# Loading the first head's operands inside the projection stage, and spreading L2 norms in fp32

## The chip, the cores and the metric

The kernel runs on one core of one Trainium2 chip. The metric is the time of one execution in microseconds of device time. Engines are named as in the profile: PE (TensorE matmuls), PEld (its weight loads), DVE (VectorE), ACT (ScalarE), POOL (GpSimd), SP (SyncE, which here issues every DMA). A DMA's time "to landing" runs from its issue to its completion.

## What is computed

Two layers run one after the other on an activation `x` of shape (2, 2048, 256) in float32. Each layer is `x = x + attention(layernorm(x)) * silu(ffn(layernorm(x)))`. There are 16 heads of width 16.

```python
# layer 0, attention: distance weights, values gated
q2, k2 = sum(Q*Q), sum(K*K)                       # per token and head
dist = sqrt(max(q2 + k2.T - 2 Q K.T, 0))
W = (1e-4 + dist) ** -2
W = W / (1e-4 + sum(W))
out = X + (G * (W V)) W_out + b_out
# layer 1, attention: cosine weights
Q, K = Q / max(norm(Q), 1e-6), K / max(norm(K), 1e-6)   # per token and head
c = clip(Q K.T, -0.999, 0.999)
W = max(1 - arccos(c) / pi, 1e-6) ** 16
W = W / (sum(W) + 1e-6)
out = (W V) Wo + bo
```

The feed-forward of each layer multiplies by ternary weights (relu squared and a low-rank term in layer 0, relu and biases in layer 1).

## The kernel before

The program is a sequence of phases, and each is one block of five engine programs with semaphores between them: `constants_phase`, then for each layer `weights_phase`, `norm_phase`, `projection_phase`, an attention phase (`distance_phase` for layer 0, `cosine_phase` for layer 1) and `output_phase`. A phase ends when all five engine programs have ended; then a short block clears its semaphores (L139 and before), and only then does the next phase begin. SP's program in a phase is one ordered list of DMA issues and waits. So a DMA that a phase needs at its start can't be issued before the phase before it has wholly ended.

**Projection.** `projection_phase` goes over the 4096 tokens in 8 blocks of 512 (`TB`), the first four of which are the first batch entry. In a block PE computes the transposed Q and K features in four tiles `ft` of 128 features (L602, two fp32 128x512 matmuls each, into the first half of `psS`), the values (and in layer 0 the gates) of four token tiles (L583, into `psM`), and the sums of squares per head (`norms`, L575, into `psO`). ACT copies each tile to `proj` (L638 or L641) and squares it (L643). DVE cuts each fp32 tile into three bf16 parts (`split_parts`, L485 to L488, two casts and two subtractions, each waiting for the one before); the parts go into one of two buffers `parts[ft % 2]`, and SP stores them to DRAM (`qk_parts`, L539). The split of a tile first waits until the store two tiles back has landed, since it overwrites that buffer. In layer 0 DVE also adds biases to values and gates (L700, L702) and splits the norms (stored at L549); after all of PE's projection work POOL sets rows 96 to 127 of all four stacks to one (L740, four memsets). SP's order in a block is: four stores of parts, the values' store (L542), in layer 0 the gates' (L545) and four stores of norm parts (L549).

In layer 1 ACT turns the sums of squares into inverse norms (L656), and they have to be spread from 8 rows per tile to 128 features. DVE clamps them (L716) and cuts them into three bf16 parts that lie in three groups of rows (L717 to L720, a chain of four); PE multiplies the parts by a bf16 selection matrix (`expand`, L592, a 32-row matmul), and DVE multiplies the projected tile by the result (L724) and splits it. In PE's order the expansion of tile `ft - 1` of block `i - 1` follows the projection of tile `ft` of block `i`, for `ft` of 1 and more, and the last follows the values.

**Attention.** For each of 32 pairs of head and batch entry (`n`), SP loads `q_stack[b]` and `k_stack[b]` (6 DMAs of 64 KB each from `qk_parts`, and in layer 0 one more for norm rows: 14 DMAs in layer 0, 12 in layer 1), then the values into `v_tile[b]`, then the feed-forward's input. PE computes scores from the stacks (L861, L1179), 16 key tiles for a pair; everything after runs on lanes of a ring. With two stacks of each kind, the loads of pair `n + 2` wait until pair `n` is done.

**Memory that is shared.** The projection's weights lie in the stacks' memory: `wqk` in `k_stack[0]`, `wvg` in `k_stack[1]`, the selection matrices `sels` in `q_stack[1]`, so no stack can be loaded while the projection runs. `woT`, needed in the output phase, lies in `q_stack[0]`.

Of the kernel before, what the change touches and what calls it, by code (L numbers as in the profile page):

```python
# [53 lines left out]
class Mem:  # L54

    def __init__(self, nc, ctx):
# [25 lines left out]
        self.woT = self.q_stack[0][:, :].bitcast(F32)[:, 0:KD * D].rearrange("p (k d) -> p k d", k=KD)  # L83
        self.wqk = self.k_stack[0][:, :].bitcast(F32).rearrange("p (k n) -> p k n", k=KD)
        self.wvg = self.k_stack[1][:, :].bitcast(F32)
        self.sels = self.q_stack[1][:, :].bitcast(F32)[:, 0:P + NCOL]
        self.later = self.q_stack[1][:, :].bitcast(F32)[:, P + NCOL:P + NCOL + 2]
        self.psS = [ctx.enter_context(nc.psum_tensor(f"psS{i}", [P, 1024], F32)) for i in range(2)]
# [106 lines left out]
def load_projection(sp, m, io, L, loaded):  # L195

    vg_w = 2 * D if L == 0 else D
    sp.dma_start(m.wqk, io[f"wqk{L}"].rearrange("(k p) n -> p k n", p=P)).then_inc(loaded, 16)
    sp.dma_start(m.wvg[:, 0:KD * vg_w].rearrange("p (k n) -> p k n", k=KD),
                 io[f"wvg{L}"].rearrange("(k p) n -> p k n", p=P)).then_inc(loaded, 16)  # L200
    sp.dma_start(m.sels[:, 0:NCOL], io["sel"]).then_inc(loaded, 16)
    sp.dma_start(m.sels[:, NCOL:NCOL + P], io["selT"]).then_inc(loaded, 16)
    if L == 1:
        sp.dma_start(m.later, io["later"]).then_inc(loaded, 16)
    return 64 + 16 * L

# [284 lines left out]
def projection_phase(nc, m, io, L):  # L491
# [12 lines left out]
    selT = m.sels[:, NCOL:NCOL + P]  # L504
    selT16 = m.work[:, 12032:12032 + P // 2].bitcast(BF16)
    r_parts = m.work[:, 11520:11776].bitcast(BF16)
    r_rest = m.area(10240, 512)
    r_high = m.work[:, 11776:12032].bitcast(BF16)
    projs = [m.area(at, NQK, 512) for at in (4096, 12288)]
# [6 lines left out]
    n_parts = m.work[:, 10752:11520].bitcast(BF16).rearrange("p (a t) -> p a t", a=3)  # L516
    r_norm = m.area(10752, 512)
    n_loads = 2
    with Phase(nc) as ctx:
# [5 lines left out]
        s_st = sems(nc, ctx, pre, "stored0", "stored1")  # L525
        s_xT, s_vst, s_ones = sems(nc, ctx, pre, "xT_stored", "values_stored", "stack_ones")
        block = ctx.block()

        @block.sync
        def _(sp):  # L530
# [29 lines left out]
        def _(pe):  # L560
            pe.sem_inc(s_nm, 1)
            if L == 1:
                pe.wait_ge(s_bias, 1)
            if L == 0:
# [22 lines left out]
            def expand(i, ft):  # L587
# [3 lines left out]
                rows = slice(ft * NCOL, (ft + 1) * NCOL)  # L591
                nc.tensor.matmul(m.psS[ft % 2][:, 512:1024], selT16[rows, :], r_parts[rows, :], start=True, stop=True)\  # L592
                    .then_inc(s_e, 1)

            for i in range(TB):
                if L == 1:
                    values(i, range(2))
                for ft in range(NQK):
# [5 lines left out]
                    if L == 0:  # L605
                        values(i, (ft,))
                    elif i > 0 and ft > 0:
                        expand(i - 1, ft - 1)
                if L == 1:
                    values(i, (2, 3))  # L610
                    if i > 0:
                        expand(i - 1, NQK - 1)
                norms(i)
# [50 lines left out]
        def _(dve):  # L664
# [7 lines left out]

            per_block = NQK * 3 + (3 if L == 0 else 4)
            chain_n = [0]
            if L == 1:
                nc.vector.tensor_copy(selT16, selT).then_inc(s_bias, 1)
            if L == 0:
# [5 lines left out]
            def dve_block(i, proj):  # L683
# [49 lines left out]
        if L == 0:  # L733
            @block.gpsimd
            def _(pool):
                pool.wait_ge(s_proj, NQK * TB)
                pool.wait_ge(s_vps, NQK * TB)
                pool.wait_ge(s_nm, TB + 1)
                for stack in m.q_stack + m.k_stack:
                    nc.gpsimd.memset(stack[ROWS:P, :], 1.0).then_inc(s_ones, 1)  # L740
                pool.wait_ge(s_ones, 2 * B)

def distance_phase(nc, m, io):
# [33 lines left out]
    with Phase(nc) as ctx:  # L778
# [12 lines left out]
        def _(sp):  # L791
# [9 lines left out]
            for n in range(TILES):  # L801
                h, b = n // B, n % B
                if n >= B:

                    sp.wait_ge(s_qk, 2 * KT * (n - 1))
                tok = slice(b * T, (b + 1) * T)
                for side, stack in ((0, m.q_stack[b]), (1, m.k_stack[b])):
                    for g, pr in enumerate(PRODUCTS):
                        at = h * DH + side * D
                        sp.dma_start(stack[g * DH:(g + 1) * DH, :], io["qk_parts"][pr[side], at:at + DH, tok])\  # L810
                            .then_inc(s_stk[b], 16)
                    at = ROWS + 3 * side
                    sp.dma_start(stack[at:at + 3, :], io["norm_parts"][:, h + HEADS * side, tok]).then_inc(s_stk[b], 16)
                if n >= B:

                    sp.wait_ge(s_pv, KT * (n - 1))
                sp.dma_start(m.v_tile[b][:, :, 0:DH], views["v_store"][:, b, :, h, :]).then_inc(s_vt[b], 16)
                if n > 0:
# [30 lines left out]
        def _(pe):  # L849
            def scores(g):  # L850
                n, kt = g // KT, g % KT
                b = n % B
                if kt == 0:
                    pe.wait_ge(s_stk[b], 16 * loads * (n // B + 1))
                for half in range(2):
# [10 lines left out]
            def weighted(g):  # L866
                n, kt = g // KT, g % KT
                b = n % B
                if kt == 0:
                    pe.wait_ge(s_vt[b], 16 * (n // B + 1))  # L870
                    if n >= B:
# [182 lines left out]
def cosine_phase(nc, m, io):  # L1054
# [45 lines left out]
    with Phase(nc) as ctx:  # L1100
# [12 lines left out]
        def _(sp):  # L1113
# [8 lines left out]
            for n in range(TILES):  # L1122
                h, b = n // B, n % B
                if n >= B:

                    sp.wait_ge(s_qk, 2 * KT * (n - 1))
                tok = slice(b * T, (b + 1) * T)
                for side, stack in ((0, m.q_stack[b]), (1, m.k_stack[b])):
                    for g, pr in enumerate(PRODUCTS):
                        at = h * DH + side * D  # L1130
                        sp.dma_start(stack[g * DH:(g + 1) * DH, :], io["qk_parts"][pr[side], at:at + DH, tok])\
                            .then_inc(s_stk[b], 16)
                if n >= B:

                    sp.wait_ge(s_pv, KT * (n - 1))
                sp.dma_start(m.v_tile[b][:, :, 0:DH], v_view[:, b, :, h, :]).then_inc(s_vt[b], 16)
                if n > 0:
# [30 lines left out]
        def _(pe):  # L1168
            def scores(g):
                h, b, kt = g // UNITS, g % UNITS // KT, g % KT  # L1170
                if kt == 0:
                    pe.wait_ge(s_stk[b], 16 * loads * (h + 1))
                for half in range(2):
# [10 lines left out]
            def weighted(g):  # L1184
                h, b, kt = g // UNITS, g % UNITS // KT, g % KT
                j, p = batch_of(g)
                if kt == 0:
                    pe.wait_ge(s_vt[b], 16 * (h + 1))
                    if h > 0:
# [353 lines left out]
def layout(inputs):  # L1543
# [8 lines left out]
    sel = np.zeros((P, NCOL), np.float32)  # L1552
    for part in range(3):
        sel[np.arange(P), part * FH + np.arange(P) // DH] = 1.0
    later = np.zeros((NQK, NCOL, 2), np.float32)
    later[:, FH:3 * FH, 0] = -1.0
    later[:, 2 * FH:3 * FH, 1] = -1.0
    arrays = {
# [10 lines left out]
        "ident": np.eye(P, dtype=np.float32), "sel": sel, "selT": np.tile(sel.T, (NQK, 1)),  # L1569
        "later": later.reshape(P, 2),  # L1570
    }
# [15 lines left out]
```

## Time and profile before

| | us |
|---|---|
| three runs | 6657.21, 6659.45, 6663.84 (median 6659.45) |
| the profiled execution | 6664.82 |
| its span in the profile | 6663.0 |
| busy in the span | ACT 6192.9 (93%), DVE 5861.2 (88%), POOL 4185.4 (63%), PE 3922.0 (59%) |
| projection, layer 0 / layer 1 | about 92 to 230 / 2261 to 2416 |
| distance / cosine phase begins | 231.6 / 2417.8 |

In a timeline each row has the start, the duration, the engine, the line and operation, what it writes and reads, how many were merged (`x4`), and in brackets how long the engine was idle before it and what ended that. SPq is SP issuing a DMA; its duration is the issue alone. A row that merges several goes from the first's start to the last's end, waits between them included. Matmul ends are modelled and can overlap the next start.

### The profile page before, as it was taken

The numbers are of one execution on the slowest core, as the hardware profiler recorded it, in microseconds if no ns is written. First come the engines' busy times: TensorE is split into PE (matmuls) and PEld (weight loads), VectorE is DVE, ScalarE is ACT, GpSimd is POOL, SyncE is SP. The second block draws the span as 40 slices with busy tenths as digits, with TensorE's granted clock in tenths as the row PEclk, the third lists the DMA queues.
The fourth block names the chain that finished last, engine by engine and source line by source line (L and its number), as shares of the span: only waits on it lengthen the run. The fifth ranks groups of instructions, "written<-read, shape, count | busy, mean of one in ns | idle before, by whom it ended". The sixth has DMA issues, their size and how long they took to land. (4 is left out here: it accounts for less than half of the span.)

```text
span 6663.0 us, 49227 instructions
## 1 busy us (share of the span) xinstructions
PE 3922.0 (59%) x17040; PEld 1374.0 (21%) x17040; DVE 5861.2 (88%) x5938; ACT 6192.9 (93%) x1955; POOL 4185.4 (63%) x1127
## 2 busy tenths in 40 slices
PE   6787778777777754544444454444445444454545
PEld 3222222222222420211111121111112111111213
DVE  7776767766777789999999999999999999999997
ACT  3699999999998449999999999999999999999996
POOL 0399999999996006565565656565565656556563
PEclk8888888888888865665556565655666565565657
DMA  3211111111112320000000000000000000000003
GB/s 138 85 27 27 20 27 25 27 27 23 24 27 60 138 76 6 15 8 9 8 15 9 8 16 8 9 8 15 9 8 16 8 9 8 15 9 8 15 6 104
DMA packets 448273, 183.51 MB, mean 28 GB/s; under 512 B 348102, under 2 KB 429913, under 8 KB 446762
## 3 DMA queue, kind: packets, MB, share of 16 engines
q1 hardware_dynamic: 448042, 180.50, 10.8%
q8 instruction: 136, 2.23, 0.1%
q14 instruction: 95, 0.78, 0.0%
HBM read 108.33 MB, written 72.09 MB: 27 GB/s over the span
## 5 line engine op out<-in xcount | busy, mean ns | idle before, releaser
L1387 POOL TENSOR_TENSOR work<-work 128x1776 f32<-128x1776 f32 (+3 forms) x696 | 2149.0, 3088 | 55.3
L1179 PE MATMUL psS<-q_stack,k_stack 96*128 96x512 bf16 x2048 | 1033.0, 607 | 1761.1 <-DVE work L1295 1695.7
L1044 POOL TENSOR_TENSOR work<-work 128x4096 f32<-128x4096 f32 x249 | 1737.7, 7013 | 154.0 <-ACT work L949 154.0
L959 DVE TENSOR_SCALAR work<-psS 128x1024 f32<-128x1024 f32 x1024 | 1200.3, 1218 | 554.1 <-PE psS L861 552.7
L1384 POOL TENSOR_SCALAR work<-work 128x1776 f32<-128x1776 f32 (+2 forms) x174 | 290.8, 1672 | 1988.4 <-ACT work L1269 1981.1
L1290 DVE TENSOR_SCALAR work<-psS 128x1024 f32<-128x1024 f32 x1024 | 1205.3, 1219 | 39.3 <-PE psS L1179 15.6
L1295 DVE TENSOR_TENSOR work<-psS,work 128x1024 f32<-128x1024 f32 x1024 | 1201.4, 1215 | 0.0
L1301 DVE SCALAR_TENSOR_TENSOR work<-work 128x2048 f32<-128x2048 f32 x512 | 1139.5, 2288 | 30.3 <-ACT work L1265 30.3
L1261 ACT ACTIVATE work<-work 128x2048 f32<-128x2048 f32 (+2 forms) x259 | 910.6, 3565 | 53.9 <-DVE work L1295 53.8
L1269 ACT ACTIVATE work<-work 128x6144 f32<-128x6144 f32 (+2 forms) x174 | 907.9, 5218 | 32.1 <-DVE work L1301 32.1
L1265 ACT ACTIVATE work<-work 128x2048 f32<-128x2048 f32 (+1 forms) x343 | 915.9, 2740 | 1.0
L944 ACT ACTIVATE work<-work 128x6144 f32<-128x6144 f32 (+1 forms) x131 | 891.1, 6865 | 13.9 <-DVE work L959 13.4
L949 ACT ACTIVATE work<-work 128x6144 f32<-128x6144 f32 (+2 forms) x133 | 891.3, 6765 | 0.5
L1198 PE MATMUL psO<-work,v_tile 128*32 128x512 f32 x4096 | 637.6, 787 | 407.7 <-issue 359.5
L879 PE MATMUL psO<-work,v_tile 128*32 128x512 f32 x4096 | 618.1, 681 | 321.9 <-POOL work L1044 315.2
L861 PE MATMUL psS<-q_stack,k_stack 102*128 102x512 bf16 x2048 | 643.8, 430 | 99.6 <-DVE work L959 73.0
L1179 PEld LDWEIGHTS psS<-q_stack,k_stack 96*128 96x128 bf16 x2048 | 133.3, 109 | 2554.4 <-DVE work L1295 2459.1
L1274 ACT ACTIVATE work<-work 128x3888 f32<-128x3888 f32 (+2 forms) x174 | 579.4, 3376 | 1.0
L1278 ACT ACTIVATE work<-work 128x3888 f32<-128x3888 f32 (+2 forms) x174 | 577.9, 3368 | 0.0
L1312 DVE TENSOR_TENSOR work<-work 128x480 f32<-128x480 f32 (+2 forms) x688 | 403.2, 657 | 0.0
L1198 PEld LDWEIGHTS psO<-work,v_tile 128*32 128x32 f32 x4096 | 169.4, 140 | 873.0 <-issue 868.2
L861 PEld LDWEIGHTS psS<-q_stack,k_stack 102*128 102x128 bf16 x2048 | 179.9, 105 | 569.2 <-DVE work L959 359.3
(150 smaller groups left out, 3432.6 us busy)
## 6 DMA issues: line engine op xcount, KB each, us to landing
qk_parts<-work SPq DMA_DIRECT2D x64, 384.0 KB, 3.3
q_stack<-qk_parts SPq DMA_DIRECT2D x384, 64.0 KB, 2.3
k_stack<-qk_parts SPq DMA_DIRECT2D x384, 64.0 KB, 2.3
xT_store<-work SPq DMA_DIRECT2D x2, 4096.0 KB, 11.4
v_store<-work SPq DMA_DIRECT2D x16, 512.0 KB, 3.5
v_tile<-v_store SPq DMA_DIRECT2D x64, 128.0 KB, 2.7
ffn_in<-xT_store SPq DMA_DIRECT2D x64, 128.0 KB, 2.7
y_store<-ffn_out SPq DMA_DIRECT2D x64, 128.0 KB, 2.4
```

The source lines that it names most:

```text
L944: nc.scalar.activation(lane(g, n), lane(g, n), ACT.Ln, scale=1.0 / (SHEP_EPS * SHEP_EPS))\
L949: nc.scalar.activation(lane(g, n), lane(g, n), ACT.Sigmoid, scale=-0.5).then_inc(s_sg, n)
L959: nc.vector.tensor_scalar(lane(g)[:, 0, half * 1024:(half + 1) * 1024], m.psS[half][:, :], ZERO_SHIFT, None, ALU.max).then_inc(s_gd, 1)
L1044: nc.gpsimd.tensor_tensor(lane(g, 2), lane(g, 2), lane(g, 2), ALU.mult).then_inc(s_wp, 1)
L1179: last = nc.tensor.matmul(m.psS[half][:, q * 512:(q + 1) * 512], m.k_stack[b][0:ROWS, kt * P:(kt + 1) * P], m.q_stack[b][0:ROWS, c:c + 512 ...
L1261: nc.scalar.activation(square(p, size), square(p, size), ACT.Ln, bias=1.0, scale=-1.0)\
L1265: nc.scalar.activation(square(p, size), square(p, size), ACT.Sigmoid, scale=-0.5)\
L1269: nc.scalar.activation(cosine(i, p, size), cosine(i, p, size), ACT.Arctan).then_inc(s_at, 1)
L1290: nc.vector.tensor_scalar(cosine(j, p)[:, 0, cols], m.psS[half][:, :], COS_MAX, -COS_MAX, ALU.min, ALU.max).then_inc(s_cl, 1)
L1295: nc.vector.tensor_tensor(square(p)[:, 0, cols], m.psS[half][:, :], cosine(j, p)[:, 0, cols], ALU.mult).then_inc(s_q, 1)
L1301: nc.vector.scalar_tensor_tensor(cosine(j, p), square(p), RSIN_MAX, cosine(j, p), ALU.min, ALU.mult).then_inc(s_z, 1)
L1387: nc.gpsimd.tensor_tensor(part, part, part, ALU.mult).then_inc(s_pp, 1)
```

## The change

The memory moves: `wqk` now lies in `k_stack[1]`, `wvg` in `q_stack[1]`, and the selection matrices in `hidden` (the feed-forward's buffer, free during projection). So stacks 0 are free while the projection runs. In both layers SP loads the stacks of the first pair between projection blocks 4 and 5, and its values at the phase's end, after all values have been stored; the phase now also waits for these loads (`first_head`), and the attention phase no longer loads or waits for pair 0. In layer 0 the memsets of stacks 0 move to the start of the phase, and those of stacks 1 stay behind the last projection (they no longer wait for the last `norms`). In layer 1 the inverse norms are no longer cut into parts: DVE only clamps them, PE spreads them in fp32, and in PE's order the expansion of tile `ft` of block `i - 1` follows the projection of tile `ft` of block `i`, `ft` of 0 included. The small array `later` and its load go, as does the cast of the selection matrix.

```diff
-        self.wqk = self.k_stack[0][:, :].bitcast(F32).rearrange("p (k n) -> p k n", k=KD)
-        self.wvg = self.k_stack[1][:, :].bitcast(F32)
-        self.sels = self.q_stack[1][:, :].bitcast(F32)[:, 0:P + NCOL]
+        self.wqk = self.k_stack[1][:, :].bitcast(F32).rearrange("p (k n) -> p k n", k=KD)
+        self.wvg = self.q_stack[1][:, :].bitcast(F32)
+        self.sels = self.hidden[:, 4:6, :].rearrange("p a b -> p (a b)")[:, 0:P + NCOL]
...
-            with sp.Fori(0, TB) as i:
+            def store_block(i):
...
+            first = TB // B
+            with sp.Fori(0, first + 1) as i:
+                store_block(i)
+            if L == 0:
+                sp.wait_ge(s_ones, 2)
+            for x in s_st:
+                sp.wait_ge(x, 16 * (2 * first + 1))
+            if L == 0:
+                sp.wait_ge(s_nst, 16 * (NQK * first + 1))
+            load_stacks(sp, m, io, L, 0, s_head)
+            with sp.Fori(first + 1, TB) as i:
+                store_block(i)
+            sp.wait_ge(s_vst, 16 * TB * (2 - L))
+            load_values(sp, m, io, 0, s_head)
+            sp.wait_ge(s_head, 16 * (2 * len(PRODUCTS) + 2 * (1 - L) + 1))
...
-                nc.tensor.matmul(m.psS[ft % 2][:, 512:1024], selT16[rows, :], r_parts[rows, :], start=True, stop=True)\
+                nc.tensor.matmul(m.psS[ft % 2][:, 512:1024], selT[rows, :], r_norm[rows, :], start=True, stop=True)\
...
-                    elif i > 0 and ft > 0:
-                        expand(i - 1, ft - 1)
+                    elif i > 0:
+                        expand(i - 1, ft)
...
-                    link(nc.vector.tensor_scalar(r_norm, n_sb, 1.0 / NORM_EPS, None, ALU.min))
-                    link(nc.vector.tensor_copy(r_high, r_norm))
-                    link(nc.vector.scalar_tensor_tensor(r_rest, r_high, m.later[:, 0:1], r_norm, ALU.mult, ALU.add))
-                    link(nc.vector.tensor_copy(r_high, r_rest))
-                    nc.vector.scalar_tensor_tensor(r_parts, r_high, m.later[:, 1:2], r_rest, ALU.mult, ALU.add)\
-                        .then_inc(s_rn, 1)
+                    nc.vector.tensor_scalar(r_norm, n_sb, 1.0 / NORM_EPS, None, ALU.min).then_inc(s_rn, 1)
...
-                pool.wait_ge(s_proj, NQK * TB)
-                pool.wait_ge(s_vps, NQK * TB)
-                pool.wait_ge(s_nm, TB + 1)
-                for stack in m.q_stack + m.k_stack:
-                    nc.gpsimd.memset(stack[ROWS:P, :], 1.0).then_inc(s_ones, 1)
+                for b in range(B):
+                    if b > 0:
+                        pool.wait_ge(s_proj, NQK * TB)
+                        pool.wait_ge(s_vps, NQK * TB)
+                    for stack in (m.q_stack[b], m.k_stack[b]):
+                        nc.gpsimd.memset(stack[ROWS:P, :], 1.0).then_inc(s_ones, 1)
...
+def load_stacks(sp, m, io, L, n, loaded):
+    h, b = n // B, n % B
+    tok = slice(b * T, (b + 1) * T)
+    for side, stack in ((0, m.q_stack[b]), (1, m.k_stack[b])):
+        for g, pr in enumerate(PRODUCTS):
+            at = h * DH + side * D
+            sp.dma_start(stack[g * DH:(g + 1) * DH, :], io["qk_parts"][pr[side], at:at + DH, tok]).then_inc(loaded, 16)
+        if L == 0:
+            at = ROWS + 3 * side
+            sp.dma_start(stack[at:at + 3, :], io["norm_parts"][:, h + HEADS * side, tok]).then_inc(loaded, 16)
```

## Rows read from the trace of the kernel before

**Rows 1.** Stretches: PE, PEld, DVE, ACT, POOL busy; clock; DMA share; GB/s.

```profile
91.50:226.80 135.30, 123.53 (x322) 50.69 (x322) 115.38 (x226) 46.91 (x72) 7.59 (x4) 0.95 0.47 158
...
2261.20:2412.00 150.80, 118.13 (x352) 54.25 (x352) 116.24 (x201) 65.92 (x112) 0.00 (x0) 0.87 0.38 133
```

**Rows 2.** Timelines of ACT and DVE, layer 0, successive blocks.

```profile
158.33 0.60 ACT L654 ACTIVATE work<-psO 128x512 f32<-128x512 f32 x1 [1.39 <-PE psO L575]
...
173.26 0.60 ACT L654 ACTIVATE work<-psO 128x512 f32<-128x512 f32 x1 [1.39 <-PE psO L575]
...
162.28 0.42 DVE L485 CAST work<-work 128x512 bf16<-128x512 f32 x1
...
177.38 0.42 DVE L485 CAST work<-work 128x512 bf16<-128x512 f32 x1
```

**Rows 3.** Timelines of SP and DVE, layer 0, blocks 4 and 5.

```profile
177.49 2.05 SPq L549 DMA_DIRECT2D norm_parts<-work  x4
180.15 9.79 SPq L539 DMA_DIRECT2D qk_parts<-work  x4
...
183.89 0.42 DVE L485 CAST work<-work 128x512 bf16<-128x512 f32 x1
```

**Rows 4.** Timeline, layer 0's projection end to first scores.

```profile
218.16 3.54 POOL L740 MEMSET q_stack<- 32x2048 bf16 x2 [217.70 <-PEq L519]
218.42 3.56 DVE L487 CAST work<-work 128x512 bf16<-128x512 f32 x1
...
223.21 0.41 DVE L702 TENSOR_TENSOR work<-psM,work 128x256 f32 x1
...
224.38 0.36 SPq L545 DMA_DIRECT2D g_store<-work  x1
224.77 1.27 DVE L487 CAST work<-work 128x512 bf16<-128x512 f32 x1
...
226.78 1.88 SPq L549 DMA_DIRECT2D norm_parts<-work  x4
231.64 2.77 SPq L810 DMA_DIRECT2D q_stack<-qk_parts  x6
...
239.34 1.89 PE L861 MATMUL psS<-q_stack,k_stack 102*128 102x512 bf16 x4 [21.37 <-DMA k_stack<-norm_parts]
```

**Rows 5.** The page's DMA issues: KB each, us to landing.

```profile
qk_parts<-work SPq DMA_DIRECT2D x64, 384.0 KB, 3.3
...
v_store<-work SPq DMA_DIRECT2D x16, 512.0 KB, 3.5
v_tile<-v_store SPq DMA_DIRECT2D x64, 128.0 KB, 2.7
```

**Rows 6.** Timeline of PE in a block of layer 1's projection.

```profile
2348.54 0.39 PE L592 MATMUL psS<-work 32*128 32x512 bf16 x1 [1.27 <-DVE work L720]
2348.86 1.98 PE L602 MATMUL psS<-work,k_stack 128*128 128x512 f32 x4
...
2358.39 3.60 PE L602 MATMUL psS<-work,k_stack 128*128 128x512 f32 x8
```

**Rows 7.** Timelines of PE and DVE, layer 1's start, middle, last block.

```profile
2262.23 3.61 PE L583 MATMUL psM<-k_stack,work 128*128 128x256 f32 x8 [2.96 <-DVE work L676]
...
2281.13 0.69 DVE L724 TENSOR_TENSOR work<-psS,work 128x512 f32<-128x512 f32 x1 [1.33 <-PE psS L592]
...
2364.71 0.60 PE L592 MATMUL psS<-work 32*128 32x512 bf16 x1 [2.72 <-DVE work L720]
...
2399.34 0.69 DVE L724 TENSOR_TENSOR work<-psS,work 128x512 f32<-128x512 f32 x1 [0.70 <-PE psS L592]
```

**Rows 8.** Timeline, layer 1's projection end to first scores.

```profile
2412.80 0.36 SPq L542 DMA_DIRECT2D v_store<-work  x1
2417.76 2.66 SPq L1131 DMA_DIRECT2D q_stack<-qk_parts  x6
...
2425.22 1.89 PE L1179 MATMUL psS<-q_stack,k_stack 96*128 96x512 bf16 x4 [21.18 <-DMA k_stack<-qk_parts]
```

More of the change, by code:

```diff
@@ L83, in __init__ @@
         self.woT = self.q_stack[0][:, :].bitcast(F32)[:, 0:KD * D].rearrange("p (k d) -> p k d", k=KD)
-        self.wqk = self.k_stack[0][:, :].bitcast(F32).rearrange("p (k n) -> p k n", k=KD)
-        self.wvg = self.k_stack[1][:, :].bitcast(F32)
-        self.sels = self.q_stack[1][:, :].bitcast(F32)[:, 0:P + NCOL]
-        self.later = self.q_stack[1][:, :].bitcast(F32)[:, P + NCOL:P + NCOL + 2]
+        self.wqk = self.k_stack[1][:, :].bitcast(F32).rearrange("p (k n) -> p k n", k=KD)
+        self.wvg = self.q_stack[1][:, :].bitcast(F32)
+        self.sels = self.hidden[:, 4:6, :].rearrange("p a b -> p (a b)")[:, 0:P + NCOL]
         self.psS = [ctx.enter_context(nc.psum_tensor(f"psS{i}", [P, 1024], F32)) for i in range(2)]
@@ L202, in load_projection @@
     sp.dma_start(m.sels[:, NCOL:NCOL + P], io["selT"]).then_inc(loaded, 16)
-    if L == 1:
-        sp.dma_start(m.later, io["later"]).then_inc(loaded, 16)
-    return 64 + 16 * L
+    return 64
 def constants_phase(nc, m, io):
@@ L504, in projection_phase @@
     selT = m.sels[:, NCOL:NCOL + P]
[L505 to L508, printed above, removed]
     projs = [m.area(at, NQK, 512) for at in (4096, 12288)]
@@ L516, in projection_phase @@
     n_parts = m.work[:, 10752:11520].bitcast(BF16).rearrange("p (a t) -> p a t", a=3)
-    r_norm = m.area(10752, 512)
+    r_norm = m.area(11520, 512)
     n_loads = 2
@@ L525, in projection_phase @@
         s_st = sems(nc, ctx, pre, "stored0", "stored1")
-        s_xT, s_vst, s_ones = sems(nc, ctx, pre, "xT_stored", "values_stored", "stack_ones")
+        s_xT, s_vst, s_ones, s_head = sems(nc, ctx, pre, "xT_stored", "values_stored", "stack_ones", "first_head")
         block = ctx.block()
@@ L561, in _ @@
             pe.sem_inc(s_nm, 1)
-            if L == 1:
-                pe.wait_ge(s_bias, 1)
             if L == 0:
@@ L606, in _ @@
                         values(i, (ft,))
-                    elif i > 0 and ft > 0:
-                        expand(i - 1, ft - 1)
+                    elif i > 0:
+                        expand(i - 1, ft)
                 if L == 1:
                     values(i, (2, 3))
-                    if i > 0:
-                        expand(i - 1, NQK - 1)
                 norms(i)
@@ L671, in _ @@
                 dve.sem_inc(x, 16)
-            per_block = NQK * 3 + (3 if L == 0 else 4)
+            per_block = NQK * 3 + (3 if L == 0 else 0)
             chain_n = [0]
-            if L == 1:
-                nc.vector.tensor_copy(selT16, selT).then_inc(s_bias, 1)
             if L == 0:
@@ L735, in _, with load_values @@
             def _(pool):
-                pool.wait_ge(s_proj, NQK * TB)
-                pool.wait_ge(s_vps, NQK * TB)
-                pool.wait_ge(s_nm, TB + 1)
-                for stack in m.q_stack + m.k_stack:
-                    nc.gpsimd.memset(stack[ROWS:P, :], 1.0).then_inc(s_ones, 1)
-                pool.wait_ge(s_ones, 2 * B)
+                for b in range(B):
[4 more added lines that the diff above has]
+                        nc.gpsimd.memset(stack[ROWS:P, :], 1.0).then_inc(s_ones, 1)
+                pool.wait_ge(s_ones, 2 * B)
+def load_stacks(sp, m, io, L, n, loaded):
[8 more added lines that the diff above has]
+            sp.dma_start(stack[at:at + 3, :], io["norm_parts"][:, h + HEADS * side, tok]).then_inc(loaded, 16)
+def load_values(sp, m, io, n, loaded):
+    h, b = n // B, n % B
+    view = io["v_store"].rearrange("p (b t) (h d) -> p b t h d", b=B, h=HEADS)
+    sp.dma_start(m.v_tile[b][:, :, 0:DH], view[:, b, :, h, :]).then_inc(loaded, 16)
 def distance_phase(nc, m, io):
@@ L805, in _ @@
                     sp.wait_ge(s_qk, 2 * KT * (n - 1))
[L806 to L813, printed above, removed]
+                if n > 0:
+                    load_stacks(sp, m, io, 0, n, s_stk[b])
                 if n >= B:
                     sp.wait_ge(s_pv, KT * (n - 1))
-                sp.dma_start(m.v_tile[b][:, :, 0:DH], views["v_store"][:, b, :, h, :]).then_inc(s_vt[b], 16)
+                if n > 0:
+                    load_values(sp, m, io, n, s_vt[b])
                 if n > 0:
@@ L852, in scores @@
                 b = n % B
-                if kt == 0:
-                    pe.wait_ge(s_stk[b], 16 * loads * (n // B + 1))
+                if kt == 0 and n > 0:
+                    pe.wait_ge(s_stk[b], 16 * loads * (n // B + b))
                 for half in range(2):
@@ L869, in weighted @@
                 if kt == 0:
-                    pe.wait_ge(s_vt[b], 16 * (n // B + 1))
+                    if n > 0:
+                        pe.wait_ge(s_vt[b], 16 * (n // B + b))
                     if n >= B:
@@ L1126, in _ @@
                     sp.wait_ge(s_qk, 2 * KT * (n - 1))
[L1127 to L1132, printed above, removed]
+                if n > 0:
+                    load_stacks(sp, m, io, 1, n, s_stk[b])
                 if n >= B:
                     sp.wait_ge(s_pv, KT * (n - 1))
-                sp.dma_start(m.v_tile[b][:, :, 0:DH], v_view[:, b, :, h, :]).then_inc(s_vt[b], 16)
+                if n > 0:
+                    load_values(sp, m, io, n, s_vt[b])
                 if n > 0:
@@ L1170, in scores @@
                 h, b, kt = g // UNITS, g % UNITS // KT, g % KT
-                if kt == 0:
-                    pe.wait_ge(s_stk[b], 16 * loads * (h + 1))
+                if kt == 0 and h + b > 0:
+                    pe.wait_ge(s_stk[b], 16 * loads * (h + b))
                 for half in range(2):
@@ L1187, in weighted @@
                 if kt == 0:
-                    pe.wait_ge(s_vt[b], 16 * (h + 1))
+                    if h + b > 0:
+                        pe.wait_ge(s_vt[b], 16 * (h + b))
                     if h > 0:
@@ L1552, in layout @@
     sel = np.zeros((P, NCOL), np.float32)
[L1553 to L1557, printed above, removed]
+    sel[np.arange(P), np.arange(P) // DH] = 1.0
     arrays = {
@@ L1569, in layout @@
         "ident": np.eye(P, dtype=np.float32), "sel": sel, "selT": np.tile(sel.T, (NQK, 1)),
-        "later": later.reshape(P, 2),
     }
```

## The prediction

> **What bounds the kernel now.** I read the stretches of the two projections first, then timelines of a middle block, then the two places where a projection hands over to its attention phase. In layer 0's projection DVE is busy 115 of 135 us and PE 124 at a granted clock of 0.95; in layer 1's it is 116 and 118 of 151 at 0.87 [rows 1]. The shares don't say which is the bound. The steps from block to block do: in layer 0 the same ACT instruction, released by PE, comes back after 14.93 us, and DVE's first cast of the norms after 15.10 [rows 2]. DVE is the slower of the two, falls 0.17 us behind in each block and has only short gaps between dependent operations. A stall of DVE in mid projection is thus paid to the phase's end. In layer 1 the first scaling of a block is at 2281.13 in the first and 2399.34 in the last block [rows 7], 16.9 us a block, while PE would need 13.45: from one block's first expansion at 2348.54 to where the next could start, 2358.39 + 3.60 [rows 6]. PE waits for DVE's chain of parts, up to 2.72 us in one place [rows 7]. So layer 1 is bound by DVE: four tiles (12.8 us: 13.46 from 2399.34 to the values' store at 2412.80 [rows 7, 8], less 0.7 for the last store of parts) and the norm chain.
>
> At both handovers everything is idle. PE waits 21.37 us in layer 0 and 21.18 in layer 1 for the last load of the first stacks [rows 4, 8]. The attention phases behind them work without a gap from the first score on (ACT is busy 93% of the span), so an earlier first score ends them earlier by as much.
>
> **Layer 0, the handover.** After the last norm parts are stored (issues 226.78 to 228.66) come the norms' landing and the change of phase, then 14 loads from 231.64, then scores at 239.34 [rows 4]. After the change one load follows the norm stores: values, issued near 228.7, landing 2.7 later [rows 5], 231.4. The change of phase costs what layer 1 shows: 2417.76 - 2412.80 = 4.96, less the landing of the values' store, 3.5 [rows 5, 8], so 1.5. (It is at most the 2.98 from 228.66 to 231.64, landing included.) Scores begin at 232.9 to 234.4; I take 233.2, a gain of 6.1 (5 to 6.4). Scores wait for no load any more; what is late next is the change of phase itself. The added wait stops SP alone, with nothing queued behind it.
>
> **Layer 0, the memsets.** DVE's cast at 218.42 takes 3.56 where others take 0.42 or 0.43 [rows 2 to 4], and ends just after POOL's two memsets of `q_stack` (218.16 + 3.54 = 221.70); the cast at 224.77 takes 1.27 beside those of `k_stack`. These are 3.1 and 0.8 us of stall on the bounding engine; some of the second is hidden, since the new load waits for the gates' store (224.38) as well, so 3.8 goes. Two memsets remain in that place, 1.8 us each or a little more, some 3.7 us in all. The two moved to the start meet no cast. The remaining pair costs 0 to 3.7; the row shows a cast that sat through two memsets, but now two casts with a subtraction of 0.7 between them share the pair, and PE ends earlier against DVE. I take 2.3. Net gain 1.5 (0 to 3.8).
>
> The Trainium skill, SBUF — State Buffer, section "SBUF: two separate sides", says that VectorE and GpSimd take a shared port pair as an exclusive lock for one whole instruction. By that rule the cast at 218.42 would have come in after the first memset, 1.5 us later and not 3.1; the row has it wait for both. By the rule the remaining pair would cost 1.5 to 2.5 and the sum would stay; if a cast sits out both, as in the row, it is 3.7 and the gain 1.4 less.
>
> **Layer 0, the loads in mid projection.** This is the price. SP issues block 4's norm stores until 177.49 + 2.05 = 179.54, and block 5's first store of parts at 180.15 [rows 3]. Between them now go 14 loads at 0.46 each (2.77 for six [rows 4]), 6.4 us, less 0.3 for the two short ones, and the waits and the second loop's start, 0.3: the store is issued near 186.0 and lands 3.3 later [rows 5], 189.3. DVE's split of tile 2, which overwrites that buffer, is due at 183.89 [rows 3]. It waits 5.4 to 5.8; loads and the landing share the engines with 1 MB of values and gates, and I take 6.2 (5 to 8). Behind the waiting split stand the value copies that free `psM`, so PE stops as well, some 3 us, which its lead covers. DVE has no slack [rows 2], so all of it is paid. Layer 0 in sum: 6.1 + 1.5 - 6.2 = 1.4 gained.
>
> **Layer 1, the projection.** PE's start loses its wait for DVE's cast of the selection matrix (2.96 idle, most of it the phase's start [rows 7]): 0.5 earlier (0 to 2.9). The first expansion comes one tile earlier in PE's order, 1.8 us (half of 3.60), but is fp32. An fp32 128x512 product takes 3.60 / 4 = 0.90, the bf16 one 0.32 from start to start or 0.39 by its row [rows 6]. The fp32 32-row product isn't in the trace: it adds 0.51 at least and 0.90 at most; I take 0.65, near the 0.58 from start to start, with something for the second weight load. So the first scaling is at 2281.13 - 0.5 - 1.8 + 0.65 = 2279.5.
>
> DVE drops four operations and keeps the clamp: its block is 12.8 + 0.5 = 13.3. PE's is 13.45 + 4 x 0.65 = 16.05 (15.5 to 17.05). The bound passes from DVE to PE, at 16.05 against 16.9 a block. The scaling of block 6 begins at 2279.5 + 6 x 16.05 = 2375.8. The last block's expansion needs no next projection: DVE ends block 6 after 12.8, clamps (0.5), PE expands (1.0): 2390.1. Before it was 2399.34: 9.2 gained (2.3 to 13).
>
> The 12 loads here cost nothing: DVE now idles 16.05 - 13.3 = 2.7 us a block for PE, so the first tile of block 5 is ready some 6.5 us after block 4 ends, and SP's 12 x 0.46 = 5.5 us, with the values' store ahead, end about then. Without that slack it would be layer 0's stall less two loads, 5.
>
> **Layer 1, the handover.** From the values' store to the first score it was 2425.22 - 2412.80 = 12.4. Now: 3.5 landing, 0.1, 2.7 for the load, 1.5 change of phase [rows 5, 8], 7.8. Gain 4.6 (3.5 to 5). Layer 1: 9.2 + 4.6 = 13.8.
>
> The memory moves and the loss of `later` with its load change nothing on the path; the selection matrices in `hidden` are read before the feed-forward writes it.
>
> **The sum.** 1.4 + 13.8 = 15.2 us off the profiled execution's 6664.8 (span 6663.0 and 1.8 around it): 6649.6. That execution was 5.4 above the median 6659.45, so the median becomes 6644.3, rounded 6645.
>
> **Rivals.**
> 1. PE is the bound in layer 1 and the fp32 expansion is dear (0.90 more than bf16, weights not hidden): 17.05 a block, so 6 us of the 9.2 are gone, gain 9, 6650. For it: the added products sit between 128-row ones and each needs its own weights. Against: weight loads lie beside products everywhere in the rows.
> 2. The 14 loads meet stores in the queue and take 10 us instead of 6.2, and layer 1's begin to stall as well: gain 9 to 11, 6649.
> 3. The transfer is hidden anyway: the stores of parts get past, and DVE doesn't wait in mid projection. Gain 21, 6638. Against it: SP issues in order.
 Against it: layer 0's projection holds 0.95 with PE busy 91% [rows 1].
> 5. The edit starts the scores earlier, but the attention phases don't end earlier, as a later load or the ring sets their pace: only the projection's 9 and 1.5 less 6.2 stay, 4 to 5 gained, 6655.
>
> **Chances.** The forecast's case has 0.66 (6641 to 6649), rival 1 0.14, rival 2 0.08, rival 3 0.05, rival 4 0.04, rival 5 0.03. 0.2% is 13.3 us, about what a measurement of this kernel tells from no change; 0.53 of the forecast's 0.66 lies beyond it. Faster: 0.53 + 0.05 = 0.58. Within: 0.13 + 0.14 + 0.08 + 0.03 = 0.38. Slower: 0.04. The range is 6638 to 6655.
>
> **What would show it.** In the profile after: in layer 0 a DVE wait of about 6 us before the cast of block 5's third tile, and only there; the last pair of memsets beside DVE's casts with at most 3.7 us lost; first scores about 6 us after the norm stores begin; in layer 1 PE without waits and the first scalings 16 us apart, DVE idle 2.7 before each; the last block's scaling 9 us earlier against the phase's start; first scores 7.8 after the values' store. It is wrong if PE's rows in layer 1 show half clock, if blocks stay 17 us apart, or if the DVE wait is far from 6.

## The result, and the profile after

The changed kernel takes 6649.4 us (median of 20 runs, 6647.2 to 6652.3), the kernel before 6661.8 (20 runs, 6657.2 to 6665.7): 12.3 us less, ratio 0.9982, 95% interval 0.9975 to 0.9988. The forecast was a gain of 15 us, a median of 6645 and a range from 6638 to 6655. The gain is just under the 13.3 us (0.2%) up to which the prediction spoke of no change; it had given 0.58 to a gain beyond that.

The profiled execution took 6648.2 (span 6646.3). The fences below are timelines of the changed kernel; columns are as in the rows of before. First come SP's rows in layer 0 between blocks 4 and 5, to be set against [rows 3]:

```profile
176.56 2.05 SPq L542 DMA_DIRECT2D norm_parts<-work  x4
178.94 2.65 SPq L749 DMA_DIRECT2D q_stack<-qk_parts  x6
...
184.64 0.30 SPq L752 DMA_DIRECT2D k_stack<-norm_parts  x1
185.29 9.48 SPq L532 DMA_DIRECT2D qk_parts<-work  x4
```

and DVE beside it:

```profile
182.63 0.41 DVE L704 TENSOR_TENSOR work<-psM,work 128x256 f32 x1
188.72 0.43 DVE L482 CAST work<-work 128x512 bf16<-128x512 f32 x1 [5.68 <-DMA qk_parts<-work]
```

The first store of parts is issued 6.35 us after the first load, and DVE's third tile waits 5.68 us for its landing. There is no other such wait in the phase. Next the end of layer 0's projection up to the first scores, against [rows 4]:

```profile
221.34 1.80 POOL L738 MEMSET q_stack<- 32x2048 bf16 x1 [127.83 <-PE psM L589]
...
222.07 1.35 DVE L482 CAST work<-work 128x512 bf16<-128x512 f32 x1
...
223.08 2.08 POOL L738 MEMSET k_stack<- 32x2048 bf16 x1
...
224.18 1.27 DVE L484 CAST work<-work 128x512 bf16<-128x512 f32 x1
...
227.85 0.36 SPq L538 DMA_DIRECT2D g_store<-work  x1
...
229.36 1.96 SPq L542 DMA_DIRECT2D norm_parts<-work  x4
231.85 0.41 SPq L759 DMA_DIRECT2D v_tile<-v_store  x1
...
236.11 1.87 PE L874 MATMUL psS<-q_stack,k_stack 102*128 102x512 bf16 x4 [13.90 <-PEq L138]
```

From the start of the last norm stores to the first scores it is 6.75 us, where it was 12.56. The casts beside the memsets lose 0.92 + 0.84 = 1.8 us, where they lost 4.0. PE in layer 1's projection, against [rows 6]:

```profile
2340.17 1.12 PE L598 MATMUL psS<-work,hidden 32*128 32x512 f32 x2
2341.22 1.98 PE L608 MATMUL psS<-work,k_stack 128*128 128x512 f32 x4
...
2356.68 1.12 PE L598 MATMUL psS<-work,hidden 32*128 32x512 f32 x2
```

PE has no wait left between these. An fp32 expansion takes 1.05 us from its start to the next product's, and a block 16.51. The stretch from the first scaling to the last block (columns as in [rows 1]) shows a granted clock of 1.00, which is the upper level, where the whole phase had 0.87 before [rows 1] and has 0.95 now:

```profile
2273.00:2389.00 116.00, 114.31 (x331) 47.31 (x329) 85.29 (x148) 55.59 (x96) 0.00 (x0) 1.00 0.39 129
```

DVE's rows in the same phase, against [rows 7], are the first scalings (`L721`) of the first block and of the last two, and one cast that waits for a store; the bracket shows how long DVE was idle before:

```profile
2275.30 0.69 DVE L721 TENSOR_TENSOR work<-psS,work 128x512 f32<-128x512 f32 x1 [2.83 <-PE psS L598]
...
2365.84 0.43 DVE L482 CAST work<-work 128x512 bf16<-128x512 f32 x1 [0.92 <-DMA qk_parts<-work]
...
2374.34 0.69 DVE L721 TENSOR_TENSOR work<-psS,work 128x512 f32<-128x512 f32 x1 [2.25 <-PE psS L598]
...
2388.75 0.69 DVE L721 TENSOR_TENSOR work<-psS,work 128x512 f32<-128x512 f32 x1 [1.21 <-PE psS L598]
```

And the phase's first DMA issue and its handover, against [rows 8]:

```profile
2257.10 0.33 SPq L528 DMA_DIRECT2D xT_store<-work  x1
...
2402.21 0.36 SPq L535 DMA_DIRECT2D v_store<-work  x1
2406.46 0.38 SPq L759 DMA_DIRECT2D v_tile<-v_store  x1
...
2410.55 1.86 PE L1190 MATMUL psS<-q_stack,k_stack 96*128 96x512 bf16 x4 [15.63 <-PEq L138]
```

**Where the time went.** Layer 0, from block 4's norm stores to the first scores: 59.55 us, before 61.85 [rows 3, 4], 2.3 less. Layer 1, from the phase's first issue (2261.16 before) to the first scores: 153.45, before 164.06, 10.6 less. Of these 6.5 lie ahead of the last block's first scaling and 4.1 behind the values' store. Together 12.9, which is the gain of the medians within its interval. The spans differ by 16.7. The other 3.8 us are no gain of the change's mechanisms: layer 0's projection begins 2.0 sooner, its part up to block 4's norm stores is 1.1 longer (its first product takes 2.07 us where it took 1.13, at a granted clock of 0.50, the lower level), the first attention phase is 0.8 shorter and all behind layer 1's first scores 2.0. Single executions of one kernel differ by more than 3.8.

### The profile page after: what moved, and what is told of

Its sections match the earlier page's. It is cut to its first block and busy times, and to the rows that moved or that the text cites. A ratio compares the mean times of both kernels' runs of the same rounds, so it can differ in the third digit from the quotient of the medians.

```text
span 6646.3 us, 49229 instructions
## 1 busy us (share of the span) xinstructions
PE 3927.5 (59%) x17072; PEld 1370.8 (21%) x17072; DVE 5838.7 (88%) x5905; ACT 6193.4 (93%) x1955; POOL 4186.6 (63%) x1127
```

## The experiments

Each is an edit of the changed kernel, but for the norms alone. The kernel before ran on the same chip in each of the three series, at a median of 6659.5 (the loads alone to the loads in two halves), 6660.3 (bf16 to all three) and 6660.8 (the memsets and the second run of all three). The ratios are against it. The changed kernel itself was timed only beside the 6661.8 above, so "less than the changed kernel" compares medians of different series. One kernel that was timed in two of them gave 6631.2 and 6634.9, so a difference of up to some 4 us between series proves nothing by itself; where the time goes is read from the stretches of the traces.

### The loads alone

The old chain of norm parts, the bf16 expansions and their old place are put back; the memory moves and the loads stay.

```diff
-                    nc.vector.tensor_scalar(r_norm, n_sb, 1.0 / NORM_EPS, None, ALU.min).then_inc(s_rn, 1)
+                    link(nc.vector.tensor_scalar(r_norm, n_sb, 1.0 / NORM_EPS, None, ALU.min))
+                    link(nc.vector.tensor_copy(r_high, r_norm))
...
-                    elif i > 0:
-                        expand(i - 1, ft)
+                    elif i > 0 and ft > 0:
+                        expand(i - 1, ft - 1)
```

> The loads and the memory moves alone, the norms' chain of parts as before. Theory A: layer 0 gains 1.2 as in the changed kernel; layer 1's handover gains 4.1 and its 12 loads fit between block 4's last store and block 5's first, since norm chain, scaling and split take some 6 us there whatever bounds the block: a wait of at most 1. Gain 4.4, 6657. Theory B, the prediction's words: without DVE's slack layer 1 stalls by 5 in mid projection, so gain about 0.3, 6661.

Measured: 6655.6 (11 runs), ratio 0.9993 (0.9984 to 1.0002). Layer 0 is as in the changed kernel (a wait of 5.59). In the trace the two stretches are 2.5 and 4.8 us shorter than before, 7.3 in sum, more than the 3.9 of the medians, whose interval takes in no change at all. Layer 1's SP, from block 4's last store to block 5's first:

```profile
2359.68 0.36 SPq L542 DMA_DIRECT2D v_store<-work  x1
2360.30 3.38 SPq L767 DMA_DIRECT2D q_stack<-qk_parts  x6
2363.72 2.74 SPq L767 DMA_DIRECT2D k_stack<-qk_parts  x6
2367.15 9.70 SPq L539 DMA_DIRECT2D qk_parts<-work  x4
```

The 12 loads fit, and DVE has no wait on a store in this phase, though it is the bound here. Theory A holds: it isn't DVE's slack that made room, but the norm chain, scaling and split, during which no store is ready. The prediction's sentence on the price without slack is wrong for this kernel (not for a faster one, below).

### The norms alone

On the kernel before: the last two edits of the change, with stacks and loads left where they were.

```diff
-                nc.tensor.matmul(m.psS[ft % 2][:, 512:1024], selT16[rows, :], r_parts[rows, :], start=True, stop=True)\
+                nc.tensor.matmul(m.psS[ft % 2][:, 512:1024], selT[rows, :], r_norm[rows, :], start=True, stop=True)\
...
-                    elif i > 0 and ft > 0:
-                        expand(i - 1, ft - 1)
+                    elif i > 0:
+                        expand(i - 1, ft)
```

> The fp32 spreading of the norms and the new place of the expansions alone, on the kernel before. Theory A: first scalings of blocks are 16.5 apart (PE without waits, each fp32 expansion 1.05 from start to start) and layer 1's projection ends 6.5 to 7 earlier: gain 7, 6655. Theory B, sizes of the prediction: 16.05 apart, 9.2 earlier, 6652.5. Theory C: the whole gain of the change comes from the handovers, this alone gives under 2.

Measured: 6654.8 (11 runs), ratio 0.9991 (0.9982 to 1.0000). In its trace scalings of successive blocks come 16.5 apart, and layer 1 takes 157.46 from first issue to first scores, 6.6 less than before. So A by the trace. The medians of the two halves (3.9 and 4.8) add to 8.7 and not 12.3; their intervals are some 6 us to each side. In the traces the halves add to 13.9 (7.3 and 6.6) against 12.9.

### Spread loads

The 14 (12) loads go behind block 5's stores of parts, up to four after each.

```diff
+                    if between is not None:
+                        for _ in range(4):
+                            next(between, None)
...
-            load_stacks(sp, m, io, L, 0, s_head)
-            with sp.Fori(first + 1, TB) as i:
+            store_block(first + 1, stack_loads(sp, m, io, L, 0, s_head))
+            with sp.Fori(first + 2, TB) as i:
```

> The changed kernel with the first stacks' loads put behind block 5's stores of parts, four by four, not all before them. Theory A (SP's order is the cause): DVE's wait of 5.68 us in layer 0 goes to under 0.5, and all of it comes off the time: 5.7 less than the changed kernel, 6643.7. Theory B (the transfers' share of the DMA engines is the cause): waits of 1 us or more remain at two to four splits, 3 us together at least, time 6646 or more. Theory C (PE would have been the bound anyway): wait gone, gain under 2, 6648.

Measured: 6643.6 (8 runs), ratio 0.9975 (0.9965 to 0.9986), 5.8 less than the changed kernel's 6649.4 (against the kernel before of each series the difference is 3.5). SP in layer 0's block 5:

```profile
178.13 0.42 SPq L532 DMA_DIRECT2D qk_parts<-work  x1
178.60 2.03 SPq L757 DMA_DIRECT2D q_stack<-qk_parts  x4
181.23 0.41 SPq L532 DMA_DIRECT2D qk_parts<-work  x1
...
184.48 0.40 SPq L532 DMA_DIRECT2D qk_parts<-work  x1
184.93 2.04 SPq L757 DMA_DIRECT2D k_stack<-qk_parts  x4
187.64 0.40 SPq L532 DMA_DIRECT2D qk_parts<-work  x1
```

Four loads take 2.0 us, and the stores of parts keep their step of 3.1 to 3.3. DVE has no wait on a store, neither here nor in layer 1, and layer 0's first scores come 54.46 after block 4's norm stores, 5.1 sooner. The same loads on the same DMA engines cost DVE nothing there. Theory A holds; B and C fall.

### Loads in two halves

Seven loads between blocks 4 and 5, seven between 5 and 6.

```diff
+            halves = stack_loads(sp, m, io, L, 0, s_head)
+            for _ in range(7 - L):
+                next(halves)
+            store_block(first + 1)
+            for _ in halves:
+                pass
```

> The changed kernel with half of the loads between blocks 4 and 5 and half between 5 and 6. Theory A (the wait is SP's issue time, one for one): two DVE waits in layer 0 of about 2.6 us each, 5.3 in all, layer 0's first scores within 1 us of the changed kernel's. Theory B (a fixed price for each interruption of SP's order): two waits of 4 or more. Theory C (a queue that fills): none or under 1 each.

Measured: one run, 6649.0. DVE's two waits in layer 0:

```profile
186.98 0.43 DVE L482 CAST work<-work 128x512 bf16<-128x512 f32 x1 [2.27 <-DMA qk_parts<-work]
...
204.09 0.43 DVE L482 CAST work<-work 128x512 bf16<-128x512 f32 x1 [1.93 <-DMA qk_parts<-work]
```

4.2 in all, where theory A had 5.3 and one batch cost 5.68. There is no fixed price, rather a free allowance at each place: seven loads take 3.0 us of SP, and the waits are 0.7 and 1.1 shorter than that. (The one batch takes 6.0 us, and 0.35 pass behind it before the next store, which the first half lacks.) First scores come 58.09 after block 4's norm stores, 1.5 sooner, the 1.5 that the waits lack. One run can't show 1.5 us in its time.

### The expansion in bf16, one part

```diff
+    selT16 = m.work[:, 12032:12032 + P // 2].bitcast(BF16)
...
-    r_norm = m.area(11520, 512)
+    r_norm = m.work[:, 11520:11776].bitcast(BF16)
...
-                nc.tensor.matmul(m.psS[ft % 2][:, 512:1024], selT[rows, :], r_norm[rows, :], start=True, stop=True)\
+                nc.tensor.matmul(m.psS[ft % 2][:, 512:1024], selT16[rows, :], r_norm[rows, :], start=True, stop=True)\
```

> The changed kernel with the inverse norms spread in bf16 as one part (their two lower parts are left out), so that only the expansion's product gets shorter. Theory A (the fp32 expansions on PE set layer 1's block time in the changed kernel): the first scalings of blocks come 13.9 to 14.2 apart and not 16.5, now set by DVE's loop of 12.8 of scaling and splitting, 0.46 clamp and 0.6 for the product; layer 1's projection is some 15 us shorter. Theory B (DVE or ACT is the bound): 16 or more apart, under 2 us gained. Theory C: PE runs at half clock after short waits, about 15 to 17 apart.

Measured: one run, 6635.1, 14.3 less. From the phase's first issue layer 1's first scores come 141.47 after, 12.0 sooner. DVE in layer 1:

```profile
2329.79 0.69 DVE L726 TENSOR_TENSOR work<-psS,work 128x512 f32<-128x512 f32 x1 [0.48 <-PE psS L601]
...
2343.46 0.69 DVE L726 TENSOR_TENSOR work<-psS,work 128x512 f32<-128x512 f32 x1 [0.48 <-PE psS L601]
...
2354.10 0.43 DVE L482 CAST work<-work 128x512 bf16<-128x512 f32 x1 [3.57 <-DMA qk_parts<-work]
```

Blocks come 13.9 apart (from 2273.85 to 2343.46 in five), so the four fp32 products set the changed kernel's 16.5. Now DVE is the bound and the chain of parts is gone too, and the loads in mid projection do cost 3.57 us in layer 1, which is why the phase is 12.0 shorter and not the 15 expected. So the loads do have a price where nothing hides it (the prediction put it at 5), and the changed kernel hides it.

### The values' load in mid projection

```diff
             load_stacks(sp, m, io, L, 0, s_head)
+            sp.wait_ge(s_vst, 16 * (first + 1) * (2 - L))
+            load_values(sp, m, io, 0, s_head)
...
-            sp.wait_ge(s_vst, 16 * TB * (2 - L))
-            load_values(sp, m, io, 0, s_head)
```

> The changed kernel with the first values' load right behind the first stacks' loads, since all its tokens are stored by then. Theory A: both handovers lose the load's 2.7 us, less 0.2 to 0.5 in layer 0 where the norms' landing is late next; DVE's wait in mid projection grows by the load's issue, 0.4. Gain 4.5 on the changed kernel: 6645. Theory B (this load's 64-byte pieces hold up the stores behind it): the wait grows by 2 or more, gain 3 or less. Theory C (the phase's end waits for something else): first scores no earlier than in the changed kernel.

Measured: 6645.9 (10 runs), ratio 0.9979 (0.9970 to 0.9988), 3.5 less than the changed kernel. DVE's waits in mid projection, layer 0 and layer 1:

```profile
189.68 0.43 DVE L482 CAST work<-work 128x512 bf16<-128x512 f32 x1 [6.58 <-DMA qk_parts<-work]
...
2367.32 0.43 DVE L482 CAST work<-work 128x512 bf16<-128x512 f32 x1 [2.55 <-DMA qk_parts<-work]
```

The waits grew by 0.9 and 1.6, between theories A and B; in layer 1 DVE's idle time takes 1.1 of the growth, and the last block's first scaling is 0.6 later. Layer 1's first scores come 5.20 after the values' store, in the changed kernel 8.34, and 2.6 sooner in sum. Layer 0's come 0.9 sooner in sum. Together that is 3.5.

### Expansions in pairs

```diff
-                    elif i > 0:
+                    elif i > 0 and ft % 2:
+                        expand(i - 1, ft - 1)
                         expand(i - 1, ft)
```

> The changed kernel with two fp32 expansions back to back (after tiles 1 and 3). Theory A (products on different row groups run side by side, as the pair at the end of the changed kernel's projection does in 1.20): PE's block falls from 16.5 to 14.6 to 14.9, the first scaling comes 1.9 later; gain 8 to 9, 6641. Theory B (they run one after the other): 16.5 apart, 2 us slower than the changed kernel, 6651. Theory C: DVE's loop is the bound above 15: gain 3 to 6.

Measured: 6642.9 (9 runs), ratio 0.9975 (0.9965 to 0.9984), 6.5 less than the changed kernel. PE, layer 1:

```profile
2306.04 1.20 PE L598 MATMUL psS<-work,hidden 32*128 32x512 f32 x4
2307.16 3.70 PE L608 MATMUL psS<-work,k_stack 128*128 128x512 f32 x8
2310.79 1.61 PE L598 MATMUL psS<-work,hidden 32*128 32x512 f32 x4
2312.34 1.99 PE L589 MATMUL psM<-q_stack,work 128*128 128x256 f32 x8
```

Two fp32 products on different groups of 32 rows take 1.12 us from the first's start to the next product's, one alone 1.05: they run side by side. The second pair takes 1.55: its second product's weights load at 2311.29, just after DVE has read that half of `psS` (a scaling from 2310.48 to 2311.17). Blocks come 14.6 apart. DVE then waits 2.85 us for a store in mid projection (0.92 in the changed kernel), and layer 1's first scores come 6.0 sooner. That wait can account for what is lacking to the 8 to 9 expected.

### All three

Spread loads, the values' load after them, and pairs.

```diff
+            def head_loads():
+                yield from stack_loads(sp, m, io, L, 0, s_head)
+                sp.wait_ge(s_vst, 16 * (first + 1) * (2 - L))
+                load_values(sp, m, io, 0, s_head)
+                yield
+
+            store_block(first + 1, head_loads())
```

> Spread loads, the values' load in mid projection and paired expansions together. Theory A: the gains add, 5.7 + 4.9 + 8.3 less than the changed kernel: 6630.5, with no DVE wait on a store in either layer. Theory B: in layer 1 the spread loads meet a DVE that is now the bound, and 1 to 3 us come back as waits: 6632 to 6634. Theory C (gains overlap, as PE becomes the bound in layer 0 too): 6637 or more.

Measured: 6631.2 (5 runs), ratio 0.9956 (0.9943 to 0.9970), and in the next series:

> The kernel with all three improvements once more, on the same chip as the one with the late memsets: 6631 as before, first scores of layer 0 as before from the projection's start (139.9 us) within 1 us; this is what the late memsets are compared with.

6634.9 (5 runs), ratio 0.9961 (0.9947 to 0.9975). The gains add within the scatter: the three alone were 5.8, 3.5 and 6.5 less than the changed kernel, 15.8 in sum, and these are 18.2 and 14.5 less; in the traces the two stretches are 16.5 and 17.4 shorter. The second series' time is 3.7 above the 6631 expected. Waits of 1.4 in layer 0's block 6 and 0.4 in layer 1 are left, which theory A had as none. In layer 0 SP then issues the values' store in 2.04 us, right behind the values' load, where it takes 0.37 with spread loads alone, and block 6's stores follow that much later:

```profile
191.01 0.39 SPq L774 DMA_DIRECT2D v_tile<-v_store  x1
191.44 2.04 SPq L538 DMA_DIRECT2D v_store<-work  x1
```

The second series' first scores come 53.43 after block 4's norm stores (139.06 after the phase's first issue, where 139.9 was expected).

### The memsets in the attention phase

As before, and POOL sets the ones of stacks 1 at the start of layer 0's attention phase; SP waits for them before pair 1's loads.

```diff
+            for stack in (m.q_stack[1], m.k_stack[1]):
+                nc.gpsimd.memset(stack[ROWS:P, :], 1.0).then_inc(s_ones, 1)
+            pool.wait_ge(s_ones, 2)
             for g in range(0, FIRST_DVE, 2):
```

> The three improvements of the kernel before this one together, and the memsets of stacks 1 moved from the end of layer 0's projection to the start of its attention phase, where POOL is idle. Theory A (a memset holds up DVE's casts and nothing else of DVE's): the stalled casts of 1.3 to 3.1 us at the end of layer 0's projection go back to 0.43, first scores come 1.8 to 2.7 us earlier, DVE's copies out of PSUM at the attention phase's start keep 1.22 us: 6629. Theory B (it holds up any DVE operation that writes SBUF): the first copies take 2 us or more, nothing gained. Theory C (the values' and gates' landing ends the phase, not the casts): under 0.5 gained.

Measured: 6631.3 (5 runs), ratio 0.9954 (0.9940 to 0.9968), 3.6 less than the kernel without this edit on the same chip. POOL, then DVE, at the attention phase's start:

```profile
229.41 1.80 POOL L1070 MEMSET q_stack<- 32x2048 bf16 x1 [133.49 <-POOLq L138]
231.15 1.80 POOL L1070 MEMSET k_stack<- 32x2048 bf16 x1
```

```profile
230.50 16.48 DVE L986 TENSOR_SCALAR work<-psS 128x1024 f32<-128x1024 f32 x14 [6.02 <-PE psS L887]
```

Fourteen copies out of PSUM take 16.48 us where two memsets run beside the first three, and the same 16.48 without them; the first three take 1.22 each in both kernels. The first scores come 51.49 after block 4's norm stores, 1.9 sooner. Theories B and C fall, and A's figures hold; its "nothing else of DVE's" doesn't, as the scaling of the biases (below) is held up too. Against the kernel before of its series this kernel is 29.6 us faster; all three improvements without it were 29.1 and 25.9.

## Why the prediction was right

Point by point, predicted and measured:

| step | predicted | measured |
|---|---|---|
| layer 0, handover | 6.1 gained | 5.8 |
| layer 0, casts beside memsets | 1.5 gained | 2.2 (4.0 less 1.8) |
| layer 0, wait in mid projection | 6.2 lost | 5.7 |
| layer 1, first scaling | 1.65 sooner | 1.8 sooner |
| layer 1, projection to the last block | 9.2 gained | 6.5 |
| layer 1, handover | 4.6 gained | 4.1 |
| sum | 15.2 | 12.9 by these stretches, 12.3 by the medians |

The number alone doesn't tell the cases apart: 6649.4 fits rival 1 (6650) and rival 2 (6649) better than the forecast's 6645. The traces do. The mechanisms are those of the forecast's case, and most were shown one by one. SP's issue order, not the transfers' traffic, makes the wait in layer 0: spreading the loads removes it. DVE's time there is paid to the end of the phase: 5.1 us of 5.7 came back in the stretch. The bound of layer 1 passes from DVE to PE: a shorter product brought the block to 13.9. And a first score that comes sooner ends the attention phase sooner: from layer 0's first scores to layer 1's projection it was 2021.8 us before and 2021.0 after (2020.4 to 2023.3 in all traces), and from layer 1's first scores to the end 4237.8 and 4235.8, so rival 5 falls. Rival 4 falls as well, with a granted clock of 1.00 in layer 1's blocks, and so does rival 3, since DVE did wait. Rival 2's 10 us of wait in layer 0 were 5.68, and layer 1's stall was 0.92. Rival 1 is half true: a block of 16.51 lies between the forecast's 16.05 and its 17.05.

The size that was off is layer 1's block on PE. I took 0.65 more for an fp32 expansion than for the bf16 one and 16.05 for a block; the expansion is 1.05 - 0.32 = 0.73 more, and a block is 16.51. Of the 0.46 the four expansions are 0.32; the other 0.14 lies in the 13.45 that I took for the rest of the block. Six blocks of 0.46 are 2.8 us, which is all that the projection fell short of 9.2. A 128-row product's 0.90 [rows 6] was thus too low for a 32-row one among them; why isn't shown. The upper bound of 0.90 extra held.

The forecast's median, 6644.3 before rounding, was 5.1 too low: 2.9 by the gain, and 2.3 since the three runs of before had a median of 6659.45 where twenty have 6661.8. That the profiled execution (6648.2) lies so near its forecast of 6649.6 is luck, as 3.8 of its gain lie outside the mechanisms.

Two smaller things were wrong. The 12 loads of layer 1 made a wait (0.92 us, taken by DVE's idle time, so they cost no time), and DVE's slack isn't the only thing that can make room for them, as the kernel with the loads alone shows. And the memsets moved to layer 0's start do meet a DVE operation, the scaling of the biases: it takes 1.87 where it took 0.17, and ends before the bias row's product that DVE waits for next (91.68 + 2.07). It begins as the first memset ends (89.96 + 1.80) and lasts until the second ends, so by these records it missed the gap between them:

```profile
91.66 1.87 DVE L681 TENSOR_SCALAR work<-work 128x2 f32<-128x2 f32 x1 [4.74 <-DMA work<-in_bvg]
91.68 2.07 PE L572 MATMUL psM<-work,ones_rows 1*128 1x512 f32 x2 [3.61 <-DMA work<-in_bvg]
91.70 1.80 POOL L738 MEMSET k_stack<- 32x2048 bf16 x1
```

For the casts, the rule of the Trainium skill (SBUF — State Buffer, "SBUF: two separate sides") fits the changed kernel: two casts were held up 0.92 and 0.84 by one memset each, 1.8 in sum, and the change's price lay in the 1.5 to 2.5 by the rule. But the row of before is no accident either: one trace of the kernel with all three improvements has a cast of 3.09 across both memsets, its other trace 1.35 and 1.26:

```profile
218.83 3.09 DVE L482 CAST work<-work 128x512 bf16<-128x512 f32 x1
```

So the 2.2 gained here against the 1.5 forecast is partly luck: with such a cast it would have been 1.3. Why a cast sometimes misses the gap between two memsets wasn't tried.

What stays open: the medians of the two halves add to 8.7 where the whole gives 12.3. The intervals allow it, and the traces of the halves show more (13.9); no run settles it.

## What to carry to other kernels

Work that is moved ahead of a phase's end pays by its place in the issuing engine's list: fourteen loads, 6.0 us of issues in one batch, held up a store that the bounding engine needed, and the same loads four at a time behind each store cost no wait. When a chain of small operations is replaced by one wider operation on another engine, count that engine's block too: here the chain's 3.0 us a block (16.9 to the 13.9 of the kernel with the short expansion) turned into only 0.4, because PE then was the bound, and pairing products on different row groups gave back most of the rest. What a handover waits for can often be loaded much sooner than its whole array is complete: the first pair's values were done at half time.

## What the runs showed of the hardware

- An fp32 product of 32 rows by 512 columns costs 1.05 us from start to start among 128-row products, a bf16 one 0.32. Two fp32 ones on different row groups, back to back, cost 1.12 together (kernel with pairs).
- A POOL memset of 32 rows by 2048 bf16 (1.8 to 2.1 us) holds up DVE's casts in SBUF (0.43 becomes 1.3 to 3.6) and its scaling of 128x2 in SBUF (0.17 becomes 1.87). It doesn't hold up DVE's subtractions in SBUF (0.69 stays, at 223.46 in the changed kernel) nor its copies out of PSUM (1.22 us each with and without).
- Loads of 64 KB take SP 0.44 to 0.46 us each to issue in layer 0's batch, up to 0.57 in layer 1's (3.42 for six). A batch of 6.0 us before a needed store became a wait of 5.68, two batches of 3.0 waits of 2.27 and 1.93.
